# Writing out the batch loops of a three-stage hybrid layer kernel on all engines

## What is computed

```
# layer 0: retention with a decay mask, 8 heads of 32
q, k, v = gn(x) @ Wq.T, gn(x) @ Wk.T * 32**-0.5, gn(x) @ Wv.T
qk  = einsum(rotate(q), rotate(k)) * mask            # mask: decay by 2-d distance, 1024 x 1024 a head
out = (qk / clip(sum|qk|, 1, 50000)) @ v
x   = x + gelu(ln_head(out)) @ Wo.T
# layer 1: causal attention, one head of 256
t   = x + softmax(causal(ln(x) @ Wq (ln(x) @ Wk).T / 16)) @ (ln(x) @ Wv)
# layer 1: eight experts, all computed, weighted by a router that looks at the mean over the batch
w   = softmax(mean_b(ln(t)) @ Wr + br)
h   = relu(bn2(relu(bn1(ln(t) @ W1[e])) @ W2[e]))
out = t + sum_e w[e] * (h @ Wo[e] + bo[e])
```

## Time and profile before

| | before |
|---|---|
| median of 3 runs | 2624.17 us (2622.93 to 2625.43) |
| the profiled execution | 2624.51 us |
| its span, first to last instruction | 2622.4 us |
| mean granted TensorE clock | 0.984 |
| TensorE matmuls busy | 2512.7 us, 96% of the span |
| VectorE busy | 1834.2 us, 70% |
| ScalarE busy | 1449.9 us, 55% |
| GpSimd busy | 517.6 us |

### The profile page before, as it was taken

One profiled execution on the slowest core, in us unless ns is written; L12 is line 12 of the kernel. 1 busy time (PEld: TensorE's weight loads), 2 busy tenths in 40 slices (PEclk: granted clock), 3 DMA queues, 4 the chain that ended last, 5 costly groups with the idle time before them and its releaser, 6 DMA issues. The chain is left out here.

```text
span 2622.4 us, 43895 instructions
## 1 busy us (share of the span) xinstructions
PE 2512.7 (96%) x15328; PEld 1786.7 (68%) x15328; DVE 1834.2 (70%) x2847; ACT 1449.9 (55%) x2044; POOL 517.6 (20%) x444
## 2 busy tenths in 40 slices
PE   5999999999999999979999969999999999999999
PEld 2444444444444444369999958888888888888888
DVE  4878777777777777657777757666666666666665
ACT  2666565566566566636566545555555555555554
POOL 2333333333333333201212110000000000000000
PEclk8999999999999999989999979999999999999999
DMA  6232222222232222123223143000000000000000
GB/s 233 51 85 60 77 62 79 65 72 75 56 85 59 83 59 70 49 71 111 82 77 115 49 146 106 18 24 24 18 23 24 24 24 24 24 24 24 24 17 16
DMA packets 116786, 157.95 MB, mean 60 GB/s; under 512 B 16272, under 2 KB 82328, under 8 KB 116384
## 3 DMA queue, kind: packets, MB, share of 16 engines
q1 hardware_dynamic: 116640, 156.01, 20.1%
HBM read 72.03 MB, written 33.59 MB: 40 GB/s over the span
## 5 line engine op out<-in xcount | busy, mean ns | idle before, releaser
L488 DVE TENSOR_TENSOR l_prod<-l_scores,l_window 128x1024 f32<-128x1024 f32 x512 | 615.6, 1218 | 220.7 <-PE l_scores L325 186.0
L679 ACT ACTIVATE l_absp<-l_prod 128x1024 f32<-128x1024 f32 x512 | 521.9, 1053 | 282.8 <-PE l_den L350 233.6
L1696 ACT ACTIVATE e_r<-e_h,e_bn,e_rs 128x512 f32<-128x512 f32 x512 | 399.4, 781 | 485.7 <-PE e_h L1547 484.5
L325 PE MATMUL l_scores<-l_qst,l_kst 96*128 96x512 f32 x1024 | 369.3, 457 | 27.9 <-DMA l_qst<-l_lo 12.0
L325 PEld LDWEIGHTS l_scores<-l_qst,l_kst 96*128 96x128 f32 x1024 | 167.4, 190 | 288.3 <-issue 147.9
L1547 PE MATMUL e_y<-e_whi,e_h2lo 128*128 128x256 f32 x1024 | 289.8, 283 | 0.0
L1546 PE MATMUL e_y<-e_wlo,e_h2hi 128*128 128x256 f32 x1024 | 289.7, 283 | 0.0
L1545 PE MATMUL e_y<-e_whi,e_h2hi 128*128 128x256 f32 x1024 | 289.2, 282 | 0.1
L350 PE MATMUL l_den<-l_absp,l_ones 128*32 128x512 f32 x2048 | 274.7, 609 | 0.0
L339 PE MATMUL l_num<-l_prod,l_v 128*32 128x512 f32 x2048 | 269.3, 598 | 0.0
L1791 DVE CAST e_h1hi<-e_r 128x512 fp32r<-128x512 f32 x256 | 111.2, 434 | 224.3 <-ACT e_r L1696 220.2
(11 more groups left out here) (191 smaller groups left out, 4472.2 us busy)
## 6 DMA issues: line engine op xcount, KB each, us to landing
l_kst<-l_hi SPq DMA_DIRECT2D x256, 64.0 KB, 2.0
l_qst<-l_hi SPq DMA_DIRECT2D x256, 64.0 KB, 2.0
l_raw<-in_xT SPq DMA_DIRECT2D x8, 1024.0 KB, 5.6
l_kst<-l_lo SPq DMA_DIRECT2D x128, 64.0 KB, 2.0
l_qst<-l_lo SPq DMA_DIRECT2D x128, 64.0 KB, 2.0
l_xo<-in_x SPq DMA_DIRECT2D x32, 256.0 KB, 2.8
x_scratch<-l_xo SPq DMA_DIRECT2D x32, 256.0 KB, 2.3
l_xr<-x_scratch SPq DMA_DIRECT2D x8, 1024.0 KB, 8.0
```

The source lines that it names most:

```text
L325: mm = nc.tensor.matmul(sc[j][:, s, :], kst[g][0:96, h, 128 * kt:128 * kt + 128], qst[c][0:96, h, :], start=True, stop=True)
L488: nc.vector.tensor_tensor(prod[n % 4][:], sc[j][:], win[:, 4 * g + 2 * j:4 * g + 2 * j + 2, w0:w0 + QC], ALU.mult).then_inc(prod_ready, 1)
L679: nc.scalar.activation(absp[n % 4][:], prod[n % 4][:], ACT.Abs).then_inc(abs_ready, 1)
L1696: nc.scalar.activation(r[m][:], p[m][:], ACT.Relu, bias=bn_[layer][1][:, m, e:e + 1], scale=rs[layer][:, m, e:e + 1]).then_inc(done, 1)
```

## The change

In each of the 15 engine programs the hardware loop becomes a Python loop, so that batches 1 to 6 are emitted one after another with b as a constant. Nothing else is touched: the same bodies, the same order of instructions, the same semaphores and the same buffers. Loop branches and the arithmetic on b are gone, and each engine's program holds every batch's instructions.

```diff
             body(0, True, False)
-            with sp.Fori(1, B - 1) as b:
+            for b in range(1, B - 1):
                 body(b, False, False)
             body(B - 1, False, True)
...
-            with pe.Fori(1, B - 1) as b:
+            for b in range(1, B - 1):
                 body(b, False, False)
...
-            with dve.Fori(1, B - 1) as b:
+            for b in range(1, B - 1):
                 body(b, False, False)
...
-            with act.Fori(1, B - 1) as b:
+            for b in range(1, B - 1):
                 body(b, False, False)
...
-            with pool.Fori(1, B - 1) as b:
+            for b in range(1, B - 1):
                 body(b, False, False)
...
             add_biases(0)
-            with pool.Fori(1, B) as b:
+            for b in range(1, B):
                 add_biases(b)
```

## The result

| | before | after |
|---|---|---|
| median | 2623.55 us (2622.75 to 2625.43, 4 runs) | 2599.52 us (2597.03 to 2602.66, 4 runs) |
| ratio | | 0.9912, 95% interval 0.9896 to 0.9927 |
| the profiled execution | 2624.51 us | 2597.03 us |
| its span | 2622.4 us | 2595.2 us |
| mean granted clock | 0.984 | 0.989 |

The kernel is faster by 24.0 us, 0.9%. The direction was right and the size was 20.3 in the forecast; 2599.5 lies 1.5 us under the range. The profiled execution after is the fastest of its four, so the traces differ by 27.2 us, more than the medians do.

What follows compares the result with a forecast made beforehand. TensorE, busy 96% of the span at almost everywhere full clock, was taken as the bound. Gains of 12.0 + 5.0 + 2.8 + 0.5 = 20.3 us from 2624.51, less 0.34, gave 2603.9 us; range 2601 to 2612.5.

Steps and rivals of the forecast that it cites:

- Part 1: TensorE's stage-1 loop: five taken back edges that wait for code fetch go, gaining 12.0 us.
- Part 2: Granted clock in stage 1: of four falls costing 1.67 us each, one stays; gain 5.0 us.
- Part 3: Register arithmetic for semaphore targets in stage-1 loops vanishes: 0.47 us a batch, 2.8 us over six.
- Part 4: Stages 2 and 3: five edges in stage 2 give 0.5 us; stage 3 gives 0.
- (a): Rival: straight code on TensorE stalls at each piece of code, stage 3 losing 86 us, near 2690; chance 0.03.
- (b): Rival: the stage-1 edge stall covers another chain that TensorE then waits for; only 3.3 us gained, 2621; chance 0.04.
- (c): Rival: the clock falls in all six middle batches of stage 1, 2612.2 us; chance 0.11, partial cases included.
- (d): Rival: waits keep their register arithmetic although the branches go, 2607.2 us; counted with the forecast's 0.82.

Runs made afterwards that it cites:

- e3: Kernel before, all loops kept, prefetch hint added to TensorE's stage-1 loop: 2607.94 us, ratio 0.9943.
- e5: Kernel before, all loops kept, TensorE's loops of stages 1 and 3 pinned to start at slot 0 of a 256-instruction piece: 2605.93 us, ratio 0.9931.
- e6: Kernel before, all loops kept, TensorE's stage-1 loop pinned to slot 128 and its stage-3 loop to slot 0: 2622.49 us, one run.
- e7: Kernel before, loops kept, TensorE's stage-1 loop pinned to slot 128 with the prefetch hint, its stage-3 loop to slot 0: 2608.32 us, one run.
- e2: Kernel before with every loop written out but TensorE's of stage 1: 2616.96 us, ratio 0.9973.
- e9: Changed kernel with VectorE's stage-1 loop put back: 2599.62 us, one run.
- e10: Changed kernel with TensorE's loops of stages 1 and 3 kept as loops, pinned to slot 0: 2601.47 us, ratio 0.9916.
- e1: Kernel before with only TensorE's stage-1 loop written out, the other fourteen kept: 2635.36 us, ratio 1.0049.

## Why the prediction was right and where it was wrong

**Part 1, the back edges: right.** The five waits are gone and each edge takes 0.97 us, so the 12.0 us are there. The stated cause, that the body is fetched afresh each time round, is confirmed by e3, e5, e6 and e7. I took it, though, for a property of the loop; it is one of the loop and its place. The 108 ns of the Trainium skill (Advanced Engine Details and Errata, Control Flow Timing) fit neither row: in the medians the branch with its code at hand took 208 to 233 ns here, the one without it 3396 to 3964. The Trainium skill's page Runtime: NRT & Kernel Launch (Instruction fetch mechanics) has the mechanism, a taken branch that waits when its target isn't held, and e6 agrees with it. But the page gives what is held as a window of 2 pages, and there the measurement decides: in e5 the branch went back over a body of seven pieces in 208 ns, with none fetched.

**Part 2, the clock: the step that failed.** I kept one fall of 1.67 us in mid-batch; the changed kernel had none in either of its two profiles. The sum had 5.0 for the clock where 6.7 was to be had in stage 1, and nothing for the passages between the stages, where the two traces differ by 2.7 + 2.7. The row of the page had shown them (the tenths of PEclk fall to 8 and 7 there), and I read it as almost everywhere full. What they give is not steady, and not shown to come from the change. In e4, the changed kernel again, the passage to stage 2 takes 55.0 us at a clock of 0.78, what it took before the change (55.3 at 0.78):

```profile
1081.20:1136.20 55.00, 35.39 (x170) 27.07 (x163) 19.99 (x46) 14.44 (x24) 8.54 (x11) 0.78 0.33 103
```

From the last exponential to the end, both profiles of the changed kernel take 1115.6 us against 1118.3 before; but e5, with all its loops, takes 1115.2, and e2, written out there as the changed kernel is, 1118.6. Without the passages the two traces differ by 21.8 us. So of the 24.0 between the medians some 2 us stand in no term that I can tie to the change. The low end of the range came from the spread of three runs, 1.3 us on either side, and was too narrow by that; thirteen runs spread by over 4 on either side.

**Part 3, registers: right in stage 1,** and for the reason given. The end of batch 6 takes 61.77 us where 61.74 was forecast, and e9 and e10 put most of the cost on VectorE. The six batches give 2.4 us where 2.8 was forecast, since the whole of batch 6 became only 0.40 shorter (132.10 to 131.70) and not 0.47.

**Part 4: stage 3 right, stage 2 under-sized.** Stage 3 stays at 133.44. Stage 2 brought 1.1 us, not 0.5: a batch went from 45.90 to 45.66 and the branch is only 0.11 of that. "Register work shows none beside it" was wrong; I had compared a looped batch with one that was looped too.

**The sum.** 20.3 was forecast. Put right from the traces it is 18.9 for edges and falls and 6 x (132.10 - 131.70) = 2.4 for registers in the six batches, 21.4 measured there; 1.1 in stage 2; 5.4 in the passages; less 0.7 net outside them, for batch 1 starts 0.9 later (172.69 against 171.76) and 0.3 of it came back in batch 7: 27.2.

**The rivals.** (a), stalls in straight code: none came up, though stage 3 now fetches all along. But it had a neighbour that I didn't think of, and e1 is it. A longer program moves the loops behind it, and stalls of over 3 us can appear where nothing was changed. With all loops written out nothing was left to be moved. (b), a covered stall: ruled out by the edges and by e5. (c), six falls: none came. (d), register arithmetic left in the waits: ruled out by the batch of 131.70 us, where e5, which has the arithmetic, takes 132.17.

## What to carry to other kernels

A loop on TensorE whose body fills seven pieces of 256 instructions or fewer ran free here (1761 and 1592 instructions; in stage 2, 681 with a branch of 215 ns), and one that touched eight without a hint paid 3.4 to 4.3 us of branch at every back edge, visible as issue waits and as instruction pieces fetched in each iteration. Look for those two rows before writing a loop out: pinning its first instruction to slot 0 or adding the prefetch hint brought 15 to 17 of the 24 us with a line or two (e3, e5). When code grows anywhere on an engine, check the branches of that engine's later loops; and give the forecast of a kernel with waits between its stages a spread from more than three executions.

## What was unexpected

- Writing out one loop made the kernel 12 us slower than before (e1, 2635.4), because another loop of the same engine had moved to a place where it is fetched anew each time: 3396 ns a branch instead of 215, and a granted clock of 0.50 behind it.
- With the hint, eight pieces are not fetched early but not fetched at all (e7: no q8 row over an iteration, branch 228 ns). So eight can be held; without the hint a ninth is fetched ahead of the branch (e6).
- A shorter branch can cost more: 2.4 us an edge in stage 1 (branch 3854 ns), 6.6 (140.07 - 133.44) in stage 3 of e1 (3396 ns), where a second piece is waited for right behind the branch, the idle stretch is 4.4 us and the clock falls after it.
